# Two PSUM copies trade engines: the attention output copy moves from ScalarE to VectorE, the transposed feed-forward input from VectorE to ScalarE

## The reference

```python
# attention, per sequence
q, k, v = split(x @ Wqkv.T)                       # 16 heads of 64, 8 chunks of 256 tokens
lam = sigmoid(relu(log(t + 1) @ Wl1.T + bl1) @ Wl2.T + bl2)
scores = einsum('bhnqd,bhnkd->bhnqk', q, k) * dh**-0.5 * lam
out = softmax(scores) @ v                         # per head and chunk
x = layernorm(x + out @ Wout.T + bout)
# feed-forward, expert 7
probs = softmax(x @ Wr.T)
y = (gelu(x @ W1[7] + b1[7]) @ W2[7] + b2[7]) * probs[:, 7:8]
x = layernorm(x + y)
```

## Time and profile before

| what | value |
|---|---|
| time, median of 3 runs | 1496.02 us (1495.59 to 1496.07) |
| the profiled execution's own time | 1492.74 us |
| its span on the slowest core (core 7) | 1491.2 us |
| spans of the eight cores | 1485.8 to 1491.2 us |
| mean granted TensorE clock of the cores | 0.807 to 0.811 |
| TensorE busy | 1106.2 us, 74% |
| VectorE busy | 510.5 us, 34% |
| ScalarE busy | 402.0 us, 27% |

### The profile page before, as it was taken

The page is one execution under the profiler, slowest core; times in us unless marked ns, Lnnn a source line. Parts: engine busy times, 40 slices in busy tenths (PEclk is TensorE's granted clock), DMA queues, the critical chain, the costliest instruction groups (busy, mean ns, idle before and its releaser), DMA issues.

```text
span 1491.2 us, 17011 instructions; the slowest of 8 cores (1485.8 to 1491.2 us)
## 1 busy us (share of the span) xinstructions
PE 1106.2 (74%) x6308; PEld 592.5 (40%) x6308; DVE 510.5 (34%) x801; ACT 402.0 (27%) x725; POOL 61.4 (4%) x118
## 2 busy tenths in 40 slices
PE   4333775877787498979786779787787598969693
PEld 0222512425152165646453415233251365636361
DVE  0344172472736502021112273544727302030303
ACT  2000141332414232232322241423324122222221
POOL 0112800000000000000000000000000000000000
PEclk9999956868586698989898857768685798979796
DMA  0566999920000520000035000000013100000001
GB/s 4 93 87 85 150 133 127 211 105 15 1 29 0 157 85 0 1 29 2 15 106 178 29 1 29 0 29 1 14 36 134 57 1 1 1 29 1 29 1 56
DMA packets 22757, 76.76 MB, mean 51 GB/s; under 512 B 3036, under 2 KB 3068, under 8 KB 19478
## 3 DMA queue, kind: packets, MB, share of 16 engines
q0 software_dynamic: 16272, 41.95, 16.1%
q1 hardware_dynamic: 6406, 33.73, 6.9%
HBM read 84.05 MB, written 25.17 MB: 73 GB/s over the span
## 4 chain that ended last, share of the span: by engine, by line
PE 50%; DVE 20%; issue 9%; DMA 8%; PEldq 5%; ACT 5%; PEld 1%; DVEq 0%; SPq 0%; ACTq 0%; POOLq 0%
PE ps L213 50%; DVE rTbf L745 13%; PEldq L245 5%; DMA stag<-wqkv 3%; DMA xf<-x 2%; DMA out<-vtok 2%; PEld ps L213 1%; DVE xT L1001 1%; DMA stag<-wout 1%; DVE aoT L762 1%; ACT vtok L683 1%; DVE kTs L655 1%; ACT L1028 1%; ACT xT L587 1%; DVE xf L855 1%
## 5 line engine op out<-in xcount | busy, mean ns | idle before, releaser
L213 PE MATMUL ps<-xT,w1a 128*128 128x256 bf16 x2048 | 287.2, 290 | 24.2 <-ACT er L1028 22.0
L213 PE MATMUL ps<-rot,hT 128*128 128x512 bf16 x1024 | 263.4, 386 | 21.6 <-DVE stzb L465 21.6
L213 PEld LDWEIGHTS ps<-xT,w1a 128*128 128x128 bf16 x2048 | 211.1, 104 | 111.5 <-issue 31.9
L745 DVE RECIPROCAL rTbf<-ps 1x256 bf16<-1x256 f32 x128 | 211.0, 1701 | 90.6 <-PE ps L213 89.7
L1066 ACT ACTIVATE hT<-ps,b1col 128x256 bf16<-128x256 f32 x256 | 120.8, 474 | 316.0 <-PE ps L213 315.7
L1001 DVE CAST xT<-ps 128x512 bf16<-128x512 f32 x32 | 21.4, 689 | 347.6 <-PE ps L213 340.9
L213 PEld LDWEIGHTS ps<-rot,hT 128*128 128x128 bf16 x1024 | 101.0, 99 | 98.1 <-issue 26.5
L213 PE MATMUL ps<-xT,rot 128*128 128x256 bf16 x1024 | 133.6, 300 | 0.0
L213 PEld LDWEIGHTS ps<-xT,rot 128*128 128x128 bf16 x1024 | 109.2, 107 | 25.5 <-issue 3.6
L721 ACT ACTIVATE eT<-ps,cconst 128x512 bf16<-128x512 f32 x128 | 87.7, 687 | 87.8 <-PE ps L213 87.7
L213 PE MATMUL ps<-eT,onesbf 128*1 128x256 bf16 x256 | 71.6, 380 | 29.6 <-ACT eT L721 23.2
(11 more groups left out here) (103 smaller groups left out, 679.4 us busy)
## 6 DMA issues: line engine op xcount, KB each, us to landing
rot<-w2img SPq DMA_DIRECT2D x16, 1024.0 KB, 14.5
xf<-x SPq DMA_DIRECT2D x16, 512.0 KB, 4.0
w1a<-w POOLq DMA_DIRECT2D x32, 256.0 KB, 26.4
w2img<-w POOLq DMA_DIRECT2D x32, 256.0 KB, 81.3
rot<-rotimg SPq DMA_DIRECT2D x8, 1024.0 KB, 6.0
stag<-wqkv POOLq DMA_DIRECT2D x24, 256.0 KB, 3.7
out<-qT POOLq DMA_DIRECT2D x8, 512.0 KB, 3.0
out<-vtok POOLq DMA_DIRECT2D x8, 512.0 KB, 2.9
```

Source lines behind the costliest of these rows:

```text
L213: return e.matmul(o, l, r, start=s_, stop=la, skip_group_check=True)
L745: e.reciprocal(rTbf(c0, 256), pk(6 + par, 0, 256, 0, 1)),
```

## The change

Two copies from PSUM swap engines; their operands, their place in the emission order and their dependencies stay. The `do_ao` copy of each head (128 in all) becomes a VectorE `tensor_copy`. The four copies to `xT` in each `b_head1` (32 in all) become ScalarE `copy` instructions. The copies to `xT` in stage A were on ScalarE already and stay there.

```diff
@@ do_ao, stage A @@
-                tok = SS(lambda e, dst=dst, par=par:
-                         e.copy(dst, pk(par, 0, 256, 0, 64)),
+                tok = VV(lambda e, dst=dst, par=par:
+                         e.tensor_copy(dst, pk(par, 0, 256, 0, 64)),
                          (prev_av[h], aoT_free), 1)
                 av_free[par] = tok
@@ b_head1, stage B @@
-                tokev = VV(lambda e, d=dst_ap, s_=src_ap: e.tensor_copy(d, s_),
+                tokev = SS(lambda e, d=dst_ap, s_=src_ap: e.copy(d, s_),
                            (mts[-1], xT_free), 1)
                 trev.append(tokev)
                 tr_free[bk] = tokev
```

## The result

The changed kernel takes 1548.39 us (median of 8 runs, 1542.59 to 1549.42); the kernel before took 1497.16 us in the runs beside it. The ratio is 1.0335, with a 95% interval of 1.0316 to 1.0355: 3.4% slower, against 3.5% forecast (1548, range 1534 to 1562).

What follows compares the result with a forecast made beforehand. VectorE was taken as the pacemaker within the heads of each tile. Heads 59.6, tile ends 0.5 and stage B -7.8 gave +52.3 us, 1545.0 from the profiled execution and 1548.3 against the median; range 1534 to 1562.

Steps and rivals of the forecast that it cites:

- The step: VectorE in the heads, from one reciprocal's start to the next with a copy between: 2.23 us in place of 1.61.
- the group: Four heads on VectorE, up to the next group's first reciprocal: 10.63 us, or +1.86; thirty-two groups give +59.6.
- No overlap between copy and reciprocal: VectorE in the heads: outputs at different partitions, so each instruction starts 0.03 us after the previous one ends.
- 1521: Rival for the heads: partition does not matter, copy and reciprocal overlap by 0.08, step 1.95 us, +25.4 in total; chance 0.06.
- three kinds of neighbours: VectorE pairs in the trace: reciprocals overlapping, reciprocal 0.03 us behind a product, start-up and norm pairs by output partition.
- One pair at start-up: VectorE at program start: outputs moving between partitions 0 and 64, second starting 0.03 us after the first (33.02 to 33.05).
- The hidden copy: Fourth copy of each group, before the bulk product: hidden by 0.07 us in VectorE's wait for the spreading matmuls.
- the tile's end: Last bulk product of a tile, waiting for the copy: 0.53 us in place of 0.46, +0.5 in all.
- Stage B: Four xT copies per tile moved to ScalarE: -7.8 us in sum; rival of no gain there, 1556, chance 0.04.
- The two first tiles: First tile of each half in stage B: copies start 2.1 and 2.45 us earlier, together -4.6.
- the chain of four copies: Stage B, first copy's start to last one's end: 3.93 us on ScalarE against 4.33, -3.2 over eight tiles.
- one more group of eight in every tile: Rival: TensorE's clock stays low longer in the projection, 1.9 us a tile, +15, 1563; clock or longer gaps 0.04.

## Why the prediction was right

**The pacemaker.** VectorE sets the heads before and after. The step was forecast at 2.23 us and measured 2.23; the copy at 0.425 and measured 0.417; the group at 10.63 and measured 10.62. Taking the copy off ScalarE gave nothing, as said.

**No overlap between copy and reciprocal.** This was the choice that decided between 1521 and 1548. It rested on three kinds of neighbours, and on the model in the Trainium skill, "VectorE: DVE Perf Modes", section on two Vector instructions with no wait between them. One pair at start-up was weaker than the prediction made it: the cast at 33.05 also reads from another partition (64) than the one ahead of it (96). The experiments leave the inputs where they were and show it in either direction: another partition for odd heads' reciprocals takes the overlap away with nothing added, and a common partition gives it back just where the two outputs start alike. By the cost table of the same page the copy would have been an estimated 0.39 us; the trace has 0.42.

**The hidden copy and the tile's end.** The wait ahead of the bulk product stayed 1.47 us. At the end of a tile the product starts 0.52 after the copy, 0.53 forecast. Heads in all: +58.6 us on average over the cores against 60.1.

**Stage B.** -7.8 forecast. The two first tiles gave 5.6 (5.3 forecast), and the chain of four copies became 0.5 shorter in each tile, not 0.4. Alone the move is worth 10 us. The remainder lies in the later tiles, the fourth of each half above all, and its cause was not traced.

**What the sum did not hold.** Projections became 5 to 7 us a core longer. The prediction had this as a rival, one more group of eight in every tile, 15 us, with a chance inside 0.04. Its price was too high: it took 1.9 us, the duration of a group at the higher clock, where a group at the lower one takes 3.57 - 1.90 = 1.67 us more. Something like it did come, in part of the tiles, but its mechanism as put there, an idler TensorE in the heads, is not supported: the kernel with doubled scores has long projections too.

It was nearly made up for by shorter stretches between tiles, -5 to -6. One reading is that the load of the next `x` is issued in the middle of the projection, and the second half of a slow projection runs beside it. In part the timelines bear this out: in the third tile of the changed kernel a core whose projection is 1 us longer has a stretch behind it that is 0.5 us shorter. But the kernels contradict it as the main cause. With filler the changed kernel's projections fell to 92.8 us and its stretches stayed short (233.9 against 233.2), and with doubled scores projections are long (102.1) and stretches too (238.5). Why the stretches became shorter stays open.

So the figure of 1548 is right partly by luck, because these two and the surplus of stage B nearly cancel: on the mean over the cores the three together come to some -2 us. The main term, the heads, was right by its mechanism.

## What to carry to other kernels

Before moving work to an engine, look at it in the stretch in question: VectorE was busy 34% of the span, and had no room at all where the copy went. The cost of an instruction is what it does to the distance between starts, not its duration: a copy of 0.42 us cost 0.62, because it also took the overlap from the two neighbours. Neighbours on VectorE whose outputs start at the same partition were cheaper here, and moving the small intermediate that `rTbf` is to another partition took no instruction more.

## What the runs showed of the hardware

- On VectorE an instruction that waits for nothing and stands behind one with another start partition of the output (0, 32 and 64 were tried) starts 0.03 us after its end. With the same start partition it starts 0.07 to 0.08 us before the end. Reciprocals of 1x256 are then 1.61 apart in place of 1.78, and from the start of a 64x256 copy from PSUM to the start of the reciprocal behind it there are 0.27 us in place of 0.45.
- TensorE's projection behind the heads ran at 1.2 GHz for one to three of its four groups of eight matmuls, and how many differs between tiles, cores and kernels: 94.9 to 96.4 us a core where the heads were as before, 100.9 to 105.2 where they were changed. With 8 or 12 filler matmuls ahead and 5 behind the drain it was 92.8 in both kernels tried.
